# The low halves of the second hidden layer subtracted on GpSimd, with new step lists for all engines

## What is computed

```python
x = x + attn_ref(cond_ref(x, cond_64, ...), W_qkv, b_qkv, ln_w, ln_b)   # experts, then banded linear attention, normalized
x = x + ffn_ref(cond2_ref(x, mask, ...), ...)                           # softmax attention, normalized, then this:

def ffn_ref(x, w1_w, w1_s, w2_w, w2_s, h1_w, h1_s, h2_w, h2_s, w3_w, w3_s):
    h = silu(tlin(x, w1_w, w1_s)) * tlin(x, w2_w, w2_s)     # 128 -> 512
    h = gelu(tlin(h, h1_w, h1_s), approximate=False)        # 512 -> 512
    h = gelu(tlin(h, h2_w, h2_s), approximate=False)        # 512 -> 512
    return tlin(h, w3_w, w3_s)                              # 512 -> 128
```

## Time and profile before

| | us |
|---|---|
| median of 3 runs (lowest to highest) | 715.75 (715.15 to 716.42) |
| profiled execution, its time | 719.08 |
| its span, first to last instruction | 717.1 |
| mean granted TensorE clock | 0.983 |

### The profile page before, as it was taken

How to read it: one execution, slowest core, us unless ns; L and a number is a source line. 1 busy time by engine, 2 the same in 40 slices (tenths; PEclk the granted TensorE clock), 3 DMA queues, 4 the chain that set the end, 5 groups by cost and what they waited for, 6 DMA issues and landing times.

```text
span 717.1 us, 20509 instructions
## 1 busy us (share of the span) xinstructions
PE 679.9 (95%) x7232; PEld 537.5 (75%) x7232; DVE 547.5 (76%) x1719; ACT 528.1 (74%) x1629; POOL 359.6 (50%) x410
## 2 busy tenths in 40 slices
...
GB/s 284 9 111 90 123 2 16 82 22 1 2 87 60 1 2 12 134 3 1 3 104 43 1 3 24 122 2 1 2 118 30 1 1 25 16 17 1 17 8 8
DMA packets 33587, 28.50 MB, mean 40 GB/s; under 512 B 4288, under 2 KB 29008, under 8 KB 33104
## 3 DMA queue, kind: packets, MB, share of 16 engines
...
...
## 4 chain that ended last, share of the span: by engine, by line
PE 57%; DVE 14%; ACT 9%; issue 7%; POOL 4%; DVEq 0%; ACTq 0%; POOLq 0%
PE ps_M L1314 30%; PE ps_z L1466 8%; DVE sb_sm L1187 5%; PE ps_S L1453 5%; PE ps_S L1438 4%; PE ps_M L1367 4%; PE ps_M L1498 3%; ACT sb_sm L830 3%; PE ps_S L1422 2%; PE ps_M L1397 2%; ACT sb_hT L795 2%; POOL sb_rq L697 1%; DVE sb_nmx L1194 1%; DVE sb_hAl L1024 1%; POOL sb_biasm L707 1%
## 5 line engine op out<-in xcount | busy, mean ns | idle before, releaser
L830 ACT ACTIVATE sb_sm<-sb_sm,sb_nmx 128x65 f32<-128x65 f32 (+3 forms) x512 | 178.1, 352 | 14.4 <-DVE sb_nmx L1194 14.1
L715 POOL TENSOR_TENSOR sb_sm<-sb_sm,sb_rden 128x128 f32<-128x128 f32 (+3 forms) x128 | 93.2, 738 | 126.4 <-DVE sb_rden L1198 126.1
L707 POOL TENSOR_TENSOR sb_biasm<-sb_bias,sb_maskn 128x128 f32<-128x128 f32 (+3 forms) x128 | 113.0, 894 | 49.6 <-DVE sb_maskn L1159 26.5
L1187 DVE SCALAR_TENSOR_TENSOR sb_sm<-ps_S,sb_rq,sb_biasm 128x65 f32<-128x65 f32 (+3 forms) x512 | 112.2, 292 | 24.0 <-PE ps_S L1438 19.5
L697 POOL TENSOR_TENSOR sb_rq<-sb_qss,sb_mhalf 128x16 f32<-128x16 f32 x32 | 93.6, 2949 | 28.8 <-DVE sb_qss L1169 28.8
L830 ACT ACTIVATION_READ_ACCUMULATOR sb_sm<-sb_sm,sb_nmx 128x1 f32 x512 | 97.1, 190 | 0.0
L1466 PE MATMUL ps_z<-sb_wout,sb_oT 128*128 128x128 f32 x512 | 69.1, 282 | 0.0
L1466 PEld LDWEIGHTS ps_z<-sb_wout,sb_oT 128*128 128x128 f32 x512 | 64.4, 193 | 4.3 <-ACT sb_oT L842 0.8
L842 ACT ACTIVATE sb_oT<-ps_S,sb_cols 128x256 f32<-128x256 f32 x128 | 52.9, 467 | 16.5 <-PE ps_S L1453 13.1
L1194 DVE TENSOR_REDUCE sb_nmx<-sb_sm 128x4 f32<-128x132 f32 (+3 forms) x128 | 59.3, 475 | 0.3
L767 ACT ACTIVATE sb_gs<-ps_M 128x512 f32<-128x512 f32 x39 | 23.2, 596 | 46.2 <-PE ps_M L1314 46.1
...
## 6 DMA issues: line engine op xcount, KB each, us to landing
...
```

What stands on the lines that cost most here:

```text
L707: pool.tensor_tensor(masked_bias(j % 4)[:, :, 1:wide], relative(bias0, i), maskn[:, j // 4, 0:wide - 1].unsqueeze(1).broadcast_to([128, 4, ...
L715: pool.tensor_tensor(p, p, stat(rden, g, j).unsqueeze(2).broadcast_to([128, 4, wide - 1]), ALU.mult)\
L830: ins = act.activation(p[:, t], p[:, t], ACT.Exp, bias=least[:, t:t + 1], accum_out=total[:, t:t + 1])
L1187: ins = dve.scalar_tensor_tensor(scored(g, j)[:, t], bank(g, "sim", n, odd)[:, first:first + wide], rq[:, col:col + 1], masked_bias(j % 4) ...
```

## The change

The subtraction `h2` moves from VectorE's list to GpSimd's, with the same waits and the same signal, and every list of the table is written anew (the same steps otherwise). Of the table, cut to the lines the text speaks of:

```diff
     "act steady": """
-        xh.0 exp.0-3 ex.0 exp.4 ex.1-2 down.0 zT.0 ex.3 qkv.0 ex.4 l1.0-1 h1.0-1 l1.2-3 h1.2-3 ex.5-7 l2.0-1
-        h2.0-1 l2.2 h2.2 l2.3 h2.3 ex.8-9 PV.0 ex.10 l3.0-1 PV.1 ln2.0 l3.2 xnT.0 l3.3 ex.11 q.0 ex.12 PV.2
...
+        xh.0 exp.0-4 ex.0-2 down.0 zT.0 ex.3 qkv.0 ex.4 l1.0-1 h1.0-1 l1.2-3 h1.2-3 ex.5-6 l2.0-1 h2.0 ex.7 h2.1
+        ex.8 PV.0 l2.2 h2.2 l2.3 h2.3 ex.9-10 l3.0 ln2.0 l3.1 xnT.0 l3.2 PV.1 l3.3 q.0 ex.11-13 PV.2 ex.14 PV.3
...
     "pool steady": """
-        zT.0 bias.4 xb.0 bias.5-6 pn.0-2 bias.7-11 pn.3-6 ln1.0 pn.7 bias.12-13 pn.8 ln2.0 bias.14 pn.9 bias.15
...
+        zT.0 bias.4 xb.0 bias.5 pn.0 bias.6 pn.1 bias.7-9 pn.2-3 bias.10-11 pn.4-5 h2.0 pn.6 bias.12-13 h2.1
+        bias.14 pn.7 ln1.0 h2.2-3 ln2.0 bias.15 pn.8-10 bias+.0-1 pn.11-13 kv.0 pn.14-15 bias+.2-3 qn.0-3
...
     "pe seventh": """
-        sim.0-1 exp.0 sim.2 exp.1-4 down.0 sim.3 zT.0 sim.4 qkv.0 scores.0 l1.0 sim.5 l1.1-3 mix.0 PV.0 l2.0
...
+        sim.0 exp.0 sim.1 exp.1 sim.2 exp.2 sim.3 exp.3-4 down.0 zT.0 qkv.0 scores.0 sim.4 l1.0-1 sim.5 l1.2-3
...
     "dve start": """
-        max.4-5 down.0 inv.2 tp.1 inv.3 sim.3 inv.4 max.6 tp.2 qkv.0 scores.0 max.7 inv.5 tp.3-4 inv.6 mix.0
-        sim.4 tp.5 max.8 inv.7 ln1.0 tp.6 max.9 sim.5 inv.8 tp.7 max.10 sim.6 max.11 inv.9-10 tp.8 xnT.0 max.12
...
+        tp.0 inv.2 tp.1 inv.3 max.5 sim.3 qkv.0 inv.4 scores.0 tp.2 max.6 inv.5 tp.3 mix.0 sim.4 max.7-8 inv.6
+        ln1.0 tp.4 max.9 inv.7 tp.5-6 sim.5 tp.7 max.10 sim.6 max.11 inv.8-10 max.12 xnT.0 tp.8-9 inv.11 max.13
...
     "sp fill": """
-        hw.0 lx.0 ls.0 vst.0 wr.0 lm.0 vb.0-1
+        ls.0 hw.0 lm.0 lx.0 vst.0 vb.0 wr.0 vb.1
```

And of the functions:

```diff
@@ block.gpsimd
+            def low2(g, o):
+                pool.wait_ge(l2_gelu.sem, l2_gelu.at(g, o + 1))
+                pool.wait_ge(l2_high.sem, l2_high.at(g, o + 1))
+                t = tokens(g)
+                pool.tensor_tensor(hBs[1][:, o, t], al[:, o % 2, t], hBs[0][:, o, t].bitcast(fp32), ALU.subtract)\
+                    .then_inc(l2_ready.sem, 1)
...
-            iterations("pool", {"xb": add_lnb, "ln1": ln1, "ln2": ln2, "kv": k_norm, "qn": q_norm,
+            iterations("pool", {"xb": add_lnb, "h2": low2, "ln1": ln1, "ln2": ln2, "kv": k_norm, "qn": q_norm,
@@ block.vector
-            def low2(g, o):
-                dve.wait_ge(l2_gelu.sem, l2_gelu.at(g, o + 1))
-                dve.wait_ge(l2_high.sem, l2_high.at(g, o + 1))
-                t = tokens(g)
-                low(hBs[1][:, o, t], al[:, o % 2, t], hBs[0][:, o, t], None, l2_ready)
-
...
-                "ln3": z_stats, "zT": ln_z, "l1": gated, "h1": low1, "h2": low2, "l4": result,
+                "ln3": z_stats, "zT": ln_z, "l1": gated, "h1": low1, "l4": result,
```

More of the change, by code:

```diff
@@ L60 @@
     "pe fill": """
-        lg.0 warm.0-2 pb.0-1 warm.3-6 rw.0 lg.1-2 exp.0-1 lg.3-4 exp.2 pb.2 lg.5-7 pb.3 exp.3-4 down.0 qkv.0
-        scores.0 mix.0 warm.7 fl.0-1 warm.8-10 fl.2 warm.11-13 xnT.0 warm.14 wr.0 warm.15-16 q.0 kv.0 q.1-4
-        qs.0-3 q.5-7 kT.0 warm.17 qs.4-7 warm.18-21
+        warm.0 lg.0 pb.0 warm.1-3 pb.1 rw.0 lg.1-2 exp.0 lg.3-4 exp.1 pb.2 lg.5 exp.2 lg.6-7 exp.3-4 pb.3 down.0
+        warm.4 qkv.0 scores.0 mix.0 warm.5 fl.0 warm.6-11 fl.1 warm.12-13 wr.0 warm.14 xnT.0 warm.15 fl.2
@@ L64 @@
+        warm.16 q.0 kv.0 q.1-4 qs.0-3 q.5-7 kT.0 warm.17 qs.4-7 warm.18-21
     """,
     "pe start": """
-        rw.0 exp.0 sim.0-1 exp.1-3 sim.2 exp.4 down.0 sim.3-4 qkv.0 scores.0 mix.0 PV.0 sim.5-6 z.0 xnT.0 PV.1
-        q.0 z.1 sim.7 z.2 kv.0 q.1 PV.2 z.3 q.2-3 z.4 PV.3 q.4 qs.0-3 q.5-7 z.5 qs.4-7 kT.0 z.6-7
+        rw.0 exp.0 sim.0 exp.1 sim.1-2 exp.2-4 down.0 sim.3-4 qkv.0 scores.0 mix.0 PV.0 sim.5-6 xnT.0 z.0-1 PV.1
+        q.0 sim.7 z.2 kv.0 q.1 z.3 PV.2 q.2-3 z.4-5 PV.3 q.4-5 qs.0-1 q.6 qs.2-3 q.7 qs.4-7 kT.0 z.6-7
@@ L68 @@
     """,
     "pe steady": """
-        sim.0 exp.0-3 sim.1 exp.4 down.0 zT.0 sim.2-3 qkv.0 l1.0 sim.4 l1.1 sim.5 l1.2-3 scores.0 l2.0-3 mix.0
-        PV.0 l3.0-2 sim.6-7 xnT.0 l3.3 kv.0 z.0 q.0 z.1 PV.1 l4.0 PV.2 q.1-2 z.2 q.3-4 qs.0-3 q.5-7 z.3 qs.4-7
-        kT.0 z.4 PV.3 z.5-7
+        sim.0 exp.0-2 sim.1 exp.3-4 down.0 zT.0 sim.2-3 qkv.0 l1.0 sim.4 l1.1-3 sim.5 scores.0 l2.0-2 mix.0 PV.0
+        l2.3 sim.6 z.0 l3.0-2 xnT.0 l3.3 q.0 sim.7 l4.0 PV.1 kv.0 z.1 q.1-2 PV.2 z.2 q.3-4 qs.0-3 q.5-7 z.3 kT.0
@@ L111 @@
     """,
     "dve fill": """
-        cg.0 pb.0 rt.0 x0.0 pb.1 rt.1-4 rw.0 pl.0 wl.0 pb.2 exp.0 pb.3 exp.1 nk.0 exp.2 rt.5 exp.3 pl.1 rt.6
-        exp.4 rt.7 down.0 xl.0 rt.8 maskn.0 qkv.0 scores.0 mix.0 pl.2 ln1.0 rt.9 xnT.0 pl.3 nk.1 q.0 kv.0 q.1-4
-        vs.0 q.5-7 ssq.0 ssc.0
+        cg.0 pb.0 rt.0 pb.1 rt.1-4 rw.0 wl.0 pl.0 x0.0 pl.1 pb.2 nk.0 exp.0 pb.3 pl.2 exp.1-2 rt.5 exp.3 rt.6
+        exp.4 rt.7 maskn.0 down.0 rt.8 qkv.0 scores.0 mix.0 ln1.0 nk.1 rt.9 xnT.0 xl.0 q.0 kv.0 pl.3 q.1-3 vs.0
@@ L116 @@
+        q.4-7 ssq.0 ssc.0
     """,
     "dve start": """
[L118 to L121 removed]
@@ L123 @@
+        q.3-6 ssq.0 ssc.0 vs.0 q.7
     """,
     "dve steady": """
-        xl.0 ln3.0 sim.0 exp.0-1 max.0-1 exp.2-3 sim.1 exp.4 max.2 zT.0 max.3 inv.0-2 down.0 zl.0 sim.2 max.4
-        tp.0-1 qkv.0 max.5 sim.3 l1.0-1 h1.0-1 inv.3 max.6 l1.2-3 max.7 inv.4 h1.2-3 scores.0 tp.2-3 sim.4 inv.5
-        max.8 inv.6 tp.4-5 sim.5 max.9 h2.0-1 max.10 inv.7 mix.0 h2.2-3 tp.6 ln1.0 inv.8-9 tp.7-8 sim.6 xnT.0
-        inv.10 max.11 tp.9 sim.7 max.12 maskn.0 max.13-14 inv.11 max.15 q.0 tp.10 inv.12 kv.0 tp.11 inv.13 l4.0
```

88 lines of the change are left out of this document (46 added, 42 removed).

## The result

The changed kernel takes **739.78 us** (median of 4 runs, 734.92 to 742.73), the kernel before beside it 716.09 (715.15 to 718.72): a ratio of 1.032, 95% interval [1.025, 1.038]. The forecast was 710.7. The profiled execution took 741.51 us.

The account below looks back on a forecast made before the run. The prediction took TensorE to bound the steady iterations, 79.64 of 80.2 us busy. Its terms summed to -5.0 us, put on the median of 715.75: 710.7 us, range 706.5 to 717.0.

Parts of the forecast that it names:

- The subtraction itself: Four subtractions per group move from VectorE to GpSimd, adding 5.2 us there per steady iteration; no cost by occupancy.
- the two engines in each other's way: Rival: GpSimd's and VectorE's SBUF reads hold each other up, +2.0 us, total 712.7; chance 0.10.
- Latency: Third layer's first output tile: the chain of low halves grows from 2.0 to 2.6 us, covered by 3.9; cost 0.
- ScalarE late at l2.3: The slower rival: table loads and softmax tiles delay ScalarE's GELUs, so TensorE waits at l3.0; 720.2 us, chance 0.17.
- The wait before xnT: Steady iterations: TensorE's 0.6 us wait before the transpose of the normed rows goes, five times; -3.0 us.
- Bank wait at l2.3: Steady iterations: the late start of the feed-forward second layer's fourth output tile, waiting for a bank, goes; -0.9 us.
- blocks: Sims split once more in five steady iterations, start, seventh and last: eight more blocks of 64x64 matmuls, 0.20 each; +1.6 us.
- Table loads: ScalarE alternates softmax and GELU more often, 63 loads against 51, 2.57 us more per steady iteration, hidden by idle time.
- Fill: GpSimd's four-column add, held by VectorE's split of wq2 in the chain mix - x1 - xnT, is no longer held; -0.9 us.
- Start: VectorE bounds the start up to xnT; two p_turns fewer stand ahead of ln1; -1.1 us.
- Seventh: Seventh stage: a sim fills TensorE's bank wait between exp.2 and exp.3; -1.0 us of a possible 0 to -2.7.
- Drain: Last group's half tiles: nothing covers the slower subtraction that TensorE's weights wait for; +0.3 us.

Follow-up runs that it names:

- e8: The changed kernel with the load of the next group's transposed inputs moved back directly behind the store of the values in SP's steady list; 731.2 us, ratio 1.018.
- e4: The kernel before with SP's fill, start and steady lists of the changed kernel; 740.6 us, ratio 1.033.
- e15: The changed kernel with the load moved back, four GELU buffers, and in the start PV.0 ahead of ex.8 and z.0 ahead of xnT; 722.7 us, ratio 1.009.
- e11: e2 with four buffers in place of two between the second layer's GELU and its low halves; 717.4 us, ratio 1.001.
- e2: The kernel before with only the third layer's low halves moved to GpSimd's list, all other lists as before; 721.1 us, ratio 1.006.
- e14: e12 with ScalarE's softmax tile ex.8 behind the third and fourth GELU, and VectorE's reciprocal inv.8 behind ln1 and sim.6; 732.6 us, ratio 1.023.
- e9: The kernel before with z.0, the output projection's first block, in front of the transpose xnT in TensorE's steady list; 718.5 us, ratio 1.002.
- e12: e8 with four buffers in place of two between the second layer's GELU and its low halves; 725.5 us, ratio 1.013.
- e1: The changed kernel with SP's fill, start and steady lists of the kernel before; 728.3 us, ratio 1.018.
- e5: The changed kernel with the fill lists of all five engines from the kernel before; 736.0 us, ratio 1.024.
- e7: e1 with two swaps in the start: PV.0 ahead of ex.8 on ScalarE, z.0 ahead of xnT on TensorE; 727.3 us, ratio 1.011.

## Why the prediction was wrong

**The step that failed** is the sentence "The four DMAs on SP's queue that change places (ls ahead of hw, lm and lx) load for the next stage; I count 0". It looked at the fill's list alone. SP's steady list, where lx falls behind the result's store (l4), the eight transfers of routing weights (wb) and a load of the values (vb), was not costed at all, and this one load is 2.3 us in each steady iteration (81.0 in e8, 83.3 on average without its edit). Put into the kernel before, SP's lists cost 24 us (e4), as much as the whole difference between the two kernels (23.7). The rows for it were there: a cover of 6.8 us, and the 5.24 us that the eight issues take. Whoever had set one against the other would have had a rival on the right side. The forecast had a slower rival, 720.2, but with another mechanism, ScalarE's.

The load alone does not put the forecast right. With it moved back e8 takes 731.2 us, and e15 with all repairs 722.7, both above the 717.0 at which the range ended. Of the 22.6 us of span, e8's move takes 10.6 (739.7 to 729.1); 4.6 are the fill, where the clock differs between executions, and 4.2 the start. The other 2.8 in the four steady iterations are the rest of the new lists, and there the sum had promised a gain: -3.0 and -0.9, against at most 1.0 for blocks, for five of them.

**The subtraction itself**: right. 1290 ns at 512 columns and 732 at 256 on GpSimd, predicted 1310 and 730; occupancy cost nothing. The rule of the Trainium skill (GPSIMD Engine Reference, 4.1 Engine selection) to keep elementwise work on VectorE agrees with 1290 against 679 ns, but in e11's steady iterations the slower engine, which has idle time, costs nothing once its buffers allow it. For the same reason the rival of the two engines in each other's way falls: e11's iterations are no longer than the kernel before's.

**Latency, "I take 0"**: wrong in its reason. The margin was worked out at TensorE's end of the chain (l3.0); the short place was ScalarE's, which waits for the ring of two. In the move alone this is 0.4 us an iteration (e2, gone in e11). Under the new lists TensorE does wait at l3.0, 0.4 us by its starts, as the rival "ScalarE late at l2.3" had it; but taking that wait away gave nothing (e14), so this rival has the place and not the price (it asked for 1.3).

**The wait before xnT, -3.0**: it went, as forecast (the 0.3 us in the changed kernel's list of waits stands before zT), and the iterations are no shorter, 81.0 in e8. e9 shows why such a wait is worth nothing: it reappears at PV.2. This was the largest term of the sum, and the error is one of kind: a wait of TensorE for a queue that is late as a whole was priced as if nothing stood behind it.

**Bank wait at l2.3, -0.9, and blocks, +1.6**: neither was tried alone. In e12's iteration no gap like the 0.41 of the earlier trace rows stands before l2.3, so the wait went; but a new 0.4 stands in layer 1. A steady iteration has seven blocks of 64x64 matmuls where it had six, as counted; in the start, which the prediction counts as an eighth, the sims stand in five blocks in both lists, so its own rule gives 7 x 0.20 = 1.4.

**Table loads, 0**: 63 loads against 51, eight in a steady iteration, as predicted, and ScalarE's 66.2 us in an iteration are the predicted 66.1; it has room for them. No experiment charged them.

**Fill, -0.9**: half right. GpSimd's add took 0.20 us and stood free, so the normalization came 0.9 earlier. But xnT did not: from mix to xnT it is 12.69 us in the kernel before and 12.60 in the changed one (12.66 in e1 and e12). TensorE's new fill list has two steps, `wr.0` and `warm.14`, in front of xnT, and the first of them waits for VectorE's routing. TensorE's timeline in the changed kernel:

```profile
62.92 0.64 PE L1354 MATMUL ps_M<-sb_ident,sb_hA 128*128 128x128 f32 x2 [4.87 <-DVE sb_route L1015]
63.36 1.06 PE L1291 MATMUL ps_S<-sb_ident 128*128 128x128 f32 x4
64.21 1.06 PE L1399 MATMUL ps_M<-sb_ident,sb_hT 128*128 128x128 f32 x4
```

ScalarE's normed rows were there at 63.3. That fill to start is 0.9 shorter in the changed kernel proves nothing: with the old fill lists the stretch is 50.3 in e2 and 50.5 in e5, with the new ones 51.2 in e1 and 51.3 in e12.

**Start, -1.1**: +4.2. The shorter queue ahead of ln1 on VectorE was real, but two places on other engines were not read: ScalarE's PV.0 behind ex.8, and xnT without z.0 in front (e7: 2.4 us).

**Seventh, -1.0**: 83.7 where it was 82.0; with SP's old lists 82.8, so 0.8 more, of which 0.7 is the one more tile of sim ahead of that point. The gap of the earlier trace rows is gone, but a sim moved there is a sim taken from between down and qkv, and TensorE now waits at that place, where it did not before:

```profile
576.47 0.50 PE L1316 MATMUL ps_M<-sb_yTh,sb_wqkvh 128*128 128x512 f32 x1 [1.23 <-DVE sb_yTl L1032]
```

In e1 that wait is 1.08. No gain is seen.

**Drain, +0.3**: from the seventh's down to the end the move alone takes 1.7 us more, 0.9 with four buffers. In the changed kernel it is 0.8, with one tile of sim (0.7) less behind that point, so some 1.5. Under-sized: the last stages have the same ring, and ScalarE waits there too.
